# Weight loads moved into the stage in front, last quad's shift on ScalarE with the routing sums, and the expert choice handed over inside its own stage

## What is computed

```python
h = _layernorm(x, axis=-1) * (1 + ca) + sa
x = x + ga * attn(h, ...)
h = _layernorm(x, axis=-1) * (1 + cb) + sb
x = x + gb * ffn(h, ...)
```

```python
main = jax.nn.gelu(x @ W1m + b1m) @ W2m + b2m
logits = jnp.mean(x, axis=1) @ w_gate + b_gate
probs = jax.nn.softmax(logits, axis=-1)
top_vals, top_idx = lax.top_k(probs, K)
gate_w = top_vals / jnp.sum(top_vals, axis=-1, keepdims=True)
...
a = jnp.clip(alpha, 0.1, 1.0)
return a * main + (1.0 - a) * expert_out
```

## Time and profile before

| | us |
|---|---|
| median of 3 runs | 6144.11 |
| lowest and highest of the runs | 6137.29, 6147.71 |
| the profiled execution's own time | 6168.16 |
| its span | 6166.0 |
| mean granted PE clock in it | 0.899 of full |

### The profile page before, as it was taken

The page is one execution under the profiler, slowest core; times in us unless marked ns, Lnnn a source line. Parts: engine busy times, 40 slices in busy tenths (PEclk is TensorE's granted clock), DMA queues, the critical chain, the costliest instruction groups (busy, mean ns, idle before and its releaser), DMA issues. The chain is left out here.

```text
span 6166.0 us, 105844 instructions
## 1 busy us (share of the span) xinstructions
PE 5082.9 (82%) x38207; PEld 2620.5 (42%) x38217; DVE 3501.2 (57%) x5633; ACT 3147.4 (51%) x7104; POOL 2512.3 (41%) x2126
## 2 busy tenths in 40 slices
PE   6999779888876999988999998874237999874995
PEld 2444334344433666643566663342112222241784
DVE  5777422487744666643666654565338999730233
ACT  2666633366663666642566663342014888831542
POOL 3333100222206888841788871116562232116025
PEclk7999989899997999998999999986557999976997
DMA  3343111133310000011000000011112333211123
GB/s 99 108 120 110 40 45 48 57 111 103 108 44 20 6 7 8 5 56 45 6 8 6 6 3 4 2 28 41 36 32 65 95 89 96 59 46 49 52 76 90
DMA packets 329515, 312.95 MB, mean 51 GB/s; under 512 B 78758, under 2 KB 279106, under 8 KB 327106
## 3 DMA queue, kind: packets, MB, share of 16 engines
q1 hardware_dynamic: 312642, 285.77, 16.2%
q0 software_dynamic: 16384, 20.69, 1.2%
HBM read 172.15 MB, written 136.32 MB: 50 GB/s over the span
## 5 line engine op out<-in xcount | busy, mean ns | idle before, releaser
L784 ACT ACTIVATE a_prob<-a_PB 128x512 f32<-128x512 f32 x2304 | 1253.4, 598 | 456.9 <-PE a_PB L626 342.7
L674 PE MATMUL a_PO<-a_prob,a_V 128*32 128x256 f32 (+3 forms) x8192 | 715.0, 422 | 22.6 <-ACT a_cn L757 22.3
L938 DVE TENSOR_REDUCE a_blocks<-a_PA 128x8 f32<-128x1024 f32 x512 | 602.0, 1214 | 37.4 <-PE a_PA L626 35.0
L941 DVE TENSOR_REDUCE a_neg<-a_PA 128x2 f32<-128x1024 f32 x512 | 590.8, 1212 | 34.8 <-PE a_PA L639 34.7
L639 PE MATMUL a_PA<-a_KS,a_QS 48*128 48x512 bf16 (+3 forms) x3072 | 469.0, 344 | 112.9 <-DVE a_blocks L938 71.0
L2538 DVE TENSOR_REDUCE f1a_neg<-f1a_PA 128x2 f32<-128x384 f32 (+1 forms) x512 | 266.7, 521 | 488.4 <-PE f1a_PA L2340 487.9
L2468 POOL TENSOR_TENSOR f1a_prob<-f1a_prob,f1a_inv 128x384 f32<-128x384 f32 (+1 forms) x512 | 394.2, 773 | 283.3 <-DVE f1a_inv L2542 283.3
L656 PE MATMUL a_PB<-a_QS,a_KS 51*128 51x512 bf16 (+3 forms) x3072 | 448.3, 329 | 56.6 <-ACT a_prob L784 54.9
L2432 ACT ACTIVATE f1a_pt<-f1a_PT 128x512 f32<-128x512 f32 (+1 forms) x512 | 278.7, 544 | 348.5 <-PE f1a_PT L2349 344.7
L2425 ACT ACTIVATE f1a_prob<-f1a_PA,f1a_neg 128x192 f32<-128x192 f32 (+1 forms) x1024 | 405.3, 404 | 67.9 <-DVE f1a_neg L2538 67.8
L639 PEld LDWEIGHTS a_PA<-a_KS,a_QS 48*128 48x128 bf16 x3072 | 123.5, 94 | 635.5 <-DVE a_blocks L938 199.6
(11 more groups left out here) (416 smaller groups left out, 10391.4 us busy)
## 6 DMA issues: line engine op xcount, KB each, us to landing
a_spill<-a_qkp SPq DMA_DIRECT2D x96, 384.0 KB
a_QS<-a_spill SPq DMA_DIRECT2D x384, 96.0 KB, 2.5
a_KS<-a_spill SPq DMA_DIRECT2D x384, 96.0 KB, 2.5
a_spill<-a_qkp SPq DMA_DIRECT2D x96, 256.0 KB
a_raw<-a_cn SPq DMA_DIRECT2D x192, 72.0 KB
a_spill<-a_qkp SPq DMA_DIRECT2D x96, 128.0 KB
f_rows<-tokens_in SPq DMA_DIRECT2D x78, 128.0 KB
tokens_out<-f_rows SPq DMA_DIRECT2D x78, 128.0 KB
```

The costliest lines, as they stand in the source:

```text
L674: mm = nc.tensor.matmul(PO[32 * j:32 * j + 32, first:last], V[:, par, t, 8 * e + pr], prob[:, k % st.ring, e, c + first - q0:c + last - q0 ...
L784: nc.scalar.activation(prob[:, k % st.ring, e], PB[:, ring_b.slot(0, ("b", s, e))], ACT.Exp, scale=scale).then_inc(pb_used, 1)
L938: nc.vector.tensor_reduce(to, of, AX, ALU.max).then_inc(pa_used, 1)
L941: nc.vector.tensor_reduce(neg[:, t, pr], PA[:, bank:bank + 2], AX, ALU.max, negate=True).then_inc(pa_used, 1)
```

## The change

Four things, in the seven norm stages, the routing and four weight-loading stages:

1. `norm_phase` gets a program for SP, which runs an optional `fetch` and waits for it at the stage's end. With it `n0b` loads the main expert and the three routing tiles, `f1n0` and `f1n1` load the GLU weights, and `n2a` loads the wide head's. The tiles are allocated around both stages, and the stages behind lose their loads and the waits on `loaded`.
2. In the six norms without `sums`, POOL adds the shift for batches 0 to 11 and ACT for the last quad.
3. In `n0b` (with `sums`) ACT adds all the shifts: quad 0 behind the copy of batch 11, quads 1 to 3 behind the last root. Each of them also writes the sum over the tokens (`accum_out`) to `route_sums`, and L1071 is gone.
4. The write to DRAM and the read back of the expert choice move from the end of the routing stage to the start of `f0`. SP reads the indices first and then the weights, and waits for both before it loads an expert; DVE waits for both before its first work in `f0`; PE and ACT wait for neither.

```diff
-def norm_phase(net, name, layer, part, small=None):
+def norm_phase(net, name, layer, part, small=None, fetch=None, sums=None):
...
+        fetched = nc.alloc_semaphore(name + "fetched")
...
+        def shift_of(b):
+            return shift[:, b:b + 1] if small is None else net.ln[:, 1, small:small + 1]
+
+        @block.sync
+        def _(sp):
+            if fetch is not None:
+                loads = fetch(sp, fetched)
+                sp.wait_ge(fetched, 16 * loads)
...
+            def add_shift(q):
+                for b in range(4 * q, 4 * q + 4):
+                    act.wait_ge(scaled, b + 1)
+                    if sums is None:
+                        nc.scalar.activation(H[:, b], h0[:, b % 4], ACT.Identity, bias=shift_of(b))
+                    else:
+                        nc.scalar.activation(H[:, b], h0[:, b % 4], ACT.Identity, bias=shift_of(b),
+                                             accum_out=sums[:, b:b + 1]).then_inc(shifted, 1)
+
             for b in range(B):
                 act.wait_ge(centered, b + 1)
                 at_least(act, variance, 4 * (b // 4 - 1))
@@ -259,7 +278,11 @@
                 nc.scalar.activation(xs[:, b], xc[:, b % 3], ACT.Copy).then_inc(taken, 1)
                 if b % 4 == 0 and b:
                     root(b // 4 - 1)
+                if b == 11 and sums is not None:
+                    add_shift(0)
             root(GROUPS - 1)
+            for q in (1, 2, 3) if sums is not None else (3,):
+                add_shift(q)
...
-            for b in range(B):
+            for b in range(B - 4 if sums is None else 0):
                 pool.wait_ge(scaled, b + 1)
-                s = shift[:, b:b + 1] if small is None else net.ln[:, 1, small:small + 1]
-                nc.gpsimd.tensor_tensor(H[:, b], h0[:, b % 4], s.broadcast_to([P, S]), ALU.add).then_inc(shifted, 1)
+                nc.gpsimd.tensor_tensor(H[:, b], h0[:, b % 4], shift_of(b).broadcast_to([P, S]), ALU.add).then_inc(shifted, 1)
...
-        @block.sync
-        def _(sp):
-            sp.dma_start(wg[:], d["f0_wg"]).then_inc(loaded, 16)
-            sp.dma_start(bg[:, 0], d["f0_bg"].partition_broadcast(B)).then_inc(loaded, 16)
-            sp.dma_start(alpha[:], d["f0_alpha"].partition_broadcast(B)).then_inc(loaded, 16)
-            sp.wait_ge(routed, 1)
-            sp.dma_start(w_dram, w[:]).then_inc(out1, 16)
-            sp.dma_start(i_dram, index[:, 0, 0:2]).then_inc(out1, 16)
-            sp.wait_ge(out1, 32)
-            sp.dma_start(net.w3[:], w_dram.rearrange("b k -> (b k)").partition_broadcast(P)).then_inc(out2, 16)
-            sp.dma_start(net.chosen[:], i_dram.rearrange("b (k o) -> o (b k)", o=1)).then_inc(out2, 16)
-            sp.wait_ge(out2, 32)
-
         @block.tensor
         def _(pe):
-            pe.wait_ge(loaded, 48)
-            pe.wait_ge(means, 2)
+            pe.wait_ge(means, 1)
             nc.tensor.matmul(ps[0:B, 0:E8], hm[:], wg[:], start=True, stop=True).then_inc(logit, 1)
...
-            nc.vector.tensor_reduce(hm[:], net.H[:], AX, ALU.add).then_inc(means, 1)
-            dve.wait_ge(means, 1)
-            nc.vector.tensor_scalar(hm[:], hm[:], 1.0 / S, None, ALU.mult).then_inc(means, 1)
+            nc.vector.tensor_scalar(hm[:], net.route_sums[:], 1.0 / S, None, ALU.mult).then_inc(means, 1)
...
-        w1 = sb("w1", [P, NU, F4 * P])
-        w2 = sb("w2", [P, NU, F4, P])
-        bias = sb("bias", [P, NU, F4 + 1])
+        w1, w2, bias = net.f0_w1, net.f0_w2, net.f0_bias
+        w_dram = nc.dram_tensor("r0_w_dram", [B, 3], F32, kind="Internal").ap()
+        i_dram = nc.dram_tensor("r0_i_dram", [B, 2], U32, kind="Internal").ap()
...
         @block.sync
         def _(sp):
-            sp.dma_start(w1[:, 0], d[name + "w1m"]).then_inc(loaded, 16)
-            sp.dma_start(w2[:, 0], d[name + "w2m"].rearrange("(t p) n -> p t n", p=P)).then_inc(loaded, 16)
-            sp.dma_start(bias[:, 0], d[name + "bm"]).then_inc(loaded, 16)
+            sp.dma_start(w_dram, net.route_w[:]).then_inc(choice_out, 16)
+            sp.dma_start(i_dram, net.route_index[:, 0, 0:2]).then_inc(choice_out, 16)
+            sp.wait_ge(choice_out, 32)
+            sp.dma_start(net.chosen[:], i_dram.rearrange("b (k o) -> o (b k)", o=1)).then_inc(choice_in, 16)
+            sp.dma_start(net.w3[:], w_dram.rearrange("b k -> (b k)").partition_broadcast(P)).then_inc(choice_in, 16)
+            sp.wait_ge(choice_in, 32)
 
             def batch(b, par):
...
         @block.tensor
         def _(pe):
-            pe.wait_ge(loaded, 48)
 
...
         @block.scalar
         def _(act):
-            act.wait_ge(loaded, 48)
...
         def _(dve):
-            dve.wait_ge(loaded, 48)
+            dve.wait_ge(choice_in, 32)
...
-        @block.sync
-        def _(sp):
-            sp.dma_start(w[:], d[name + "w"].rearrange("j p n -> p j n")).then_inc(loaded, 16)
-
         @block.tensor
         def _(pe):
-            pe.wait_ge(loaded, 16)
...
         @block.sync
         def _(sp):
-            sp.dma_start(w1[:], d["f1_w1"][l].rearrange("p (j n) -> p j n", n=P)).then_inc(loaded, 16)
-            sp.dma_start(w2[:], d["f1_w2"][l].rearrange("(j p) n -> p j n", p=P)).then_inc(loaded, 16)
-            sp.dma_start(b1[:], d["f1_b1"][l]).then_inc(loaded, 16)
-            sp.dma_start(b2[:], d["f1_b2"][l]).then_inc(loaded, 16)
             if not last:
                 sp.wait_ge(zeroed, 1)
...
         @block.tensor
         def _(pe):
-            pe.wait_ge(loaded, 64)
...
@@ -2720,9 +2705,22 @@
         for l in range(2):
             with nc.cleanup_on_exit():
                 local_attention_phase(net, f"f1a{l}_", l)
-            with nc.sbuf_tensor(f"N{l}", [P, B, S], F32) as net.N:
+            with ExitStack() as own:
+                net.N = own.enter_context(nc.sbuf_tensor(f"N{l}", [P, B, S], F32))
+                net.glu_w1 = own.enter_context(nc.sbuf_tensor(f"glu{l}_w1", [P, 2 * GLU, P], F32))
+                net.glu_w2 = own.enter_context(nc.sbuf_tensor(f"glu{l}_w2", [P, GLU, P], F32))
+                net.glu_b1 = own.enter_context(nc.sbuf_tensor(f"glu{l}_b1", [P, 2 * GLU], F32))
+                net.glu_b2 = own.enter_context(nc.sbuf_tensor(f"glu{l}_b2", [P, 1], F32))
+
+                def fetch(sp, fetched):
+                    sp.dma_start(net.glu_w1[:], net.d["f1_w1"][l].rearrange("p (j n) -> p j n", n=P)).then_inc(fetched, 16)
+                    sp.dma_start(net.glu_w2[:], net.d["f1_w2"][l].rearrange("(j p) n -> p j n", p=P)).then_inc(fetched, 16)
+                    sp.dma_start(net.glu_b1[:], net.d["f1_b1"][l]).then_inc(fetched, 16)
+                    sp.dma_start(net.glu_b2[:], net.d["f1_b2"][l]).then_inc(fetched, 16)
+                    return 4
+
                 with nc.cleanup_on_exit():
-                    norm_phase(net, f"f1n{l}_", 1, 1, small=l)
+                    norm_phase(net, f"f1n{l}_", 1, 1, small=l, fetch=fetch)
                 with nc.cleanup_on_exit():
                     glu_phase(net, f"f1g{l}_", l, last=(l == 1))
 
@@ -2771,21 +2769,43 @@
             modulation_phase(net)
         with nc.cleanup_on_exit():
             heads16_phase(net, "a0_", 0, causal=True, rope=True, w_sum=False)
-        with nc.cleanup_on_exit():
-            norm_phase(net, "n0b_", 0, 1)
-        with nc.cleanup_on_exit():
-            route_batches_phase(net)
-        with nc.cleanup_on_exit():
-            mlp_phase(net, "f0_", 0, 3)
+        with ExitStack() as own:
+            def sb(n, shape, dt=F32):
+                return own.enter_context(nc.sbuf_tensor(n, shape, dt))
+
+            net.route_wg, net.route_bg, net.route_alpha = sb("route_wg", [P, E8]), sb("route_bg", [B, 1, E8]), sb("route_alpha", [B, 1])
+            net.route_index, net.route_w, net.route_sums = sb("route_index", [B, 1, E8], U32), sb("route_w", [B, 3]), sb("route_sums", [P, B])
+            net.f0_w1, net.f0_w2, net.f0_bias = sb("f0_w1", [P, 3, F4 * P]), sb("f0_w2", [P, 3, F4, P]), sb("f0_bias", [P, 3, F4 + 1])
+
+            def fetch_main(sp, fetched):
+                sp.dma_start(net.route_wg[:], d["f0_wg"]).then_inc(fetched, 16)
+                sp.dma_start(net.route_bg[:, 0], d["f0_bg"].partition_broadcast(B)).then_inc(fetched, 16)
+                sp.dma_start(net.route_alpha[:], d["f0_alpha"].partition_broadcast(B)).then_inc(fetched, 16)
+                sp.dma_start(net.f0_w1[:, 0], d["f0_w1m"]).then_inc(fetched, 16)
+                sp.dma_start(net.f0_w2[:, 0], d["f0_w2m"].rearrange("(t p) n -> p t n", p=P)).then_inc(fetched, 16)
+                sp.dma_start(net.f0_bias[:, 0], d["f0_bm"]).then_inc(fetched, 16)
+                return 6
+
+            with nc.cleanup_on_exit():
+                norm_phase(net, "n0b_", 0, 1, fetch=fetch_main, sums=net.route_sums)
+            with nc.cleanup_on_exit():
+                route_batches_phase(net)
+            with nc.cleanup_on_exit():
+                mlp_phase(net, "f0_", 0, 3)
         with nc.cleanup_on_exit():
```

(13 more changed lines are left out.)

28 lines of the change are left out of this document (8 added, 20 removed).

## The result

The changed kernel takes **6120.7 us** (median of seven runs, 6113.4 to 6131.5) against 6144.1 before (6137.3 to 6155.0): a ratio of 0.9959, with an interval from 0.9947 to 0.9970, so 25 us less (18 to 33). Two repeats of the same comparison gave 0.9948 (0.9935 to 0.9962) and 0.9948 (0.9930 to 0.9966), each on another chip. The forecast was 6111.0, a ratio of 0.9946, in a range of 6101 to 6122. Sign and range held; the first comparison is 10 us short of the forecast, the two repeats are not.

The account below looks back on a forecast made before the run. No engine bounds the whole kernel; stages differ, with dead time at norm ends, weight-load starts and routing. Terms 8.3 + 0.8 + 8.65 + 2.9 + 12.5 = 33.1 us, off 6144.1, gave 6111.0, range 6101 to 6122.

Parts of the forecast that it names:

- Tails of six norms: Ends of six norms: ACT takes POOL's last quad and ends 0.75 us behind DVE, 1.38 us each, 8.3 us together.
- Tail of `n0b`: End of `n0b`: ACT adds with accumulator reads and ends earlier, 0.8 us won, between 0.4 and 1.2.
- The price of nothing: Middle of `n0b`: quad 0's additions on ACT cost nothing, covered by DVE's 1.91 us idle; otherwise up to 3.6 us.
- Routing: Routing stage: removing the sum at L1071 takes 8.69 us off the only path; counted as 8.65 us.
- Start of `f0`: First expert's product in `f0` comes 5.1 us earlier, less 2.2 for a second cold start: 2.9 us, ends 2.7 and 5.1.
- Start of three more stages: GLU 0, GLU 1 and wide head: PE no longer waits for loads, 4.47, 5.29 and 2.70 us, together 12.5.
- nothing is added: Starts of both GLU stages and wide head: PE cold before and cold again, so no extra cost, 0 us.
- (a): Stage starts: another wait of PE replaces the load wait, 6117 us, or 6123.5 if all 12.5 stayed; chance 9%.
- (b): `f0`: the clock stays up over the idle time, gain 5.1 instead of 2.9 us, total 6108.8; chance 8%.
- (c): Norm tails: ACT reloads its table for the new additions, 1.28 us in each of seven, total 6120; chance 2%.
- (d): `f0`: PE stays at the lower clock after its second start, total 6156 us or more; chance 2%.
- (e): Untouched stages run otherwise against the clock's changes; a loss of 21 us or more hides the gain, about 6135; chance 4%.

Follow-up runs that it names:

- The part alone: Only the last quad's shift moved from POOL to ACT in all seven norms, against the kernel before: 5964.7 us, ratio 0.9983.
- the trace where the yardstick was 18.32: Whole change, third time, against the kernel before: 6124.8 us, ratio 0.9948; yardstick: routing's last result to first product of L1155 (L1157 after the change).
- the fillers in the hole: Twenty useless products on PE in f0's idle stretch, added to the changed kernel and nothing else: 5948.4 us in one run (before on that chip: 5973.8).
- the three traces of the table: Stage-by-stage traces of the whole change, unaltered, against two of the kernel before; measured 6120.7, 5944.2 and 6124.8 us, ratios 0.9959, 0.9948 and 0.9948.
- The products in the norm: Useless bf16 products on PE in the last third of every norm, added to the changed kernel: 6118.3 us, ratio to before 0.9935.

## Why the prediction came out as it did

**Tails of six norms: right.** Forecast 1.38 each, from ACT 0.75 us behind DVE. It is 0.75 to 0.76 us in the six norms of the changed kernel. The part alone gave 10 us in total against 9.7 expected with `n0b`'s part.

**Tail of `n0b`: right within its bounds, at the upper one.** The read of the accumulator overlaps but for the last, so the tail shrank by 2.13 - 0.98 = 1.15 us; I had taken 0.8 between 0.4 and 1.2. One sign that I had named failed: DVE's idle time of 1.91 us before the reciprocal of quad 3 did not shrink, it vanished (762.20 has no bracket). The working had a slip there: 3.6 us behind 761.96 is 765.6, not 765, so the reciprocal of quad 2 could have come 2.3 us late, more than the cover of 1.91. The price of nothing held only because ACT's additions were cheaper than the 0.91 us taken: in the middle of the norm the four with their reads hold ACT up for 2.8 us (751.89 to 754.71), 0.7 each. They did push DVE, by the new wait of 0.56 us at 756.38. Before quad 3 the cover was then used up but not exceeded: ACT's root ends at 761.41 + 0.69 = 762.10 in the changed kernel, and DVE goes from its product to the reciprocal at 762.20 without a pause.

**Routing: right.** Forecast 8.65. From DVE's first instruction to the last result it was 797.10 - 784.84 = 12.26 us and is 778.41 - 774.78 = 3.63: 8.63 less.

**Start of `f0`: the mechanism was right, two sizes were off.** Forecast 2.9, measured 19.0 - 17.0 = 2.0 to 2.1 us. The step "the expert's last tile is issued at 805.09", 7.99 us behind the last result, came true to 0.03 us (786.37 - 778.41 = 7.96; 8.1 and 8.5 in the other two traces of it). The step "lands 2.6 us later" failed: PE started 3.48 us behind that issue (786.37 to 789.85), and 2.6 and 3.4 us behind it in the other two traces. I had taken the median over all 32 loads of the stage for the first one. So the hole was 5.0 us long, not 3.7, and by the prediction's own sign ("wrong if that hole is longer" than 3 to 4 us) this step failed. The second cold start came, and cost 5.40 - 3.70 = 1.7 us here, where the lower level lasted 3.4 us, and 6.57 - 3.70 = 2.9 in the trace where the yardstick was 18.32 and it lasted 6.8; I had taken 2.2. The Trainium skill ("TensorE: Matmul & The Clock Gate", section "HAM oscillation — how this bites in real kernels") was right against this edit, and the fillers in the hole show the size of it. What I had not weighed is that leaving the hand-over outside would have brought as much: the edit won 6 us in PE's start and paid them back in the hole and in the second cold start.

**Start of three more stages: the waits were right, "nothing is added" failed.** The time from DVE's end to PE's start shrank by 16.6 us over the three (16.9 in the first pair of traces) against 12.5 + 3 x 1.38 = 16.6 forecast. But the stages themselves grew by 2.5, of which 2.3 in the two GLU stages. "PE was cold at these starts and will be cold again, so nothing is added" took both cold starts for equally long. With the old starts the GLU stages ran at the lower level for 3.5 to 5.1 us (eight starts in four traces, mean 4.0). With the new ones it was 3.0 to 6.2 us (fourteen starts in seven traces, mean 5.0), 5.9 in the mean of the three traces of the table. Each us more at the lower level costs half a us. So the three traces of the table lie above the rest: over all seven with the new starts the two GLU stages take 256.6 us in the mean, over the four with the old ones 255.5, which makes the term 1.1 us and not 2.3.

The granted clock shows where the level comes from. It does not fall at the GLU stage's first product; it has fallen in the norm, 15.4 to 17.0 us before that product with the old starts and 9.5 to 12.4 us before it with the new ones. The whole stretch at the lower level lasted 20.5 us at each of the eight old starts, 17.1 at eleven of the new ones and 13.7 at three. PE's start comes some 6 us earlier and the stretch ends 3.4 us earlier at eleven starts and 6.8 at three, so mostly more of it lies behind the start. The products in the norm remove it: at five of the six GLU starts behind them the clock is full well before the first product, at the sixth from 1.3 us before it. What decides between 13.7 and 17.1 us was not tried.

**The sum.** 33.1 forecast, 31.9 by the stages, 31 and 33 us by the two later comparisons, 25 by the first. Added up from what the steps measured it is less: six tails 8.2, `n0b` 1.15, routing 8.6, `f0` 2.1, the waits 12.5, less 2.3 in the GLU stages, together 30.3. The other 1.6 of the 31.9 no step explains; they are within what traces scatter (`n0b` alone took 44.0 us in one trace of before and 41.0 in the other), so that the stages came so near the forecast is in part luck. The first comparison's interval ends at 33. The profiled pair of the first comparison can't decide it: its spans differ by 47.5 us, of which only 34.0 lie in the touched stages. The 10 us between forecast and first result stay open, as scatter that I can't assign. (The low end of the sum, 31.2, does not follow from the bounds given for its terms; they give 31.85.)

**The rivals.** (a) fell: PE starts 0.76 us behind ACT. (b) fell: the clock is at 0.56 in the first 2 us behind the hole, and the eight products there take 5.40 us. (c) fell: ACT's table is loaded at 774.74 and 779.11, at the stages' starts, and nowhere in a norm's tail; the kernel has 24 table loads before and after. (d) fell: the product behind them, L1157, takes its 3.60 us, the time at full clock, and `f0` as a whole has a clock of 0.99 as before:

```profile
779.20:1128.00 348.80, 338.17 (x768) 145.05 (x768) 74.89 (x96) 133.19 (x193) 0.00 (x0) 0.99 0.17 49
```

(e) fell as a large effect: the untouched attention stages differ by -0.6 us in the means. But one of them, behind an unchanged border, is longer, which the prediction had named as a sign against it. The second local-attention stage takes either 832.4 to 833.1 us or 835.2 to 836.1. It was the short time in both traces of the kernel before, and the long one in all three of the changed kernel, 3.4 us more; the kernels with a part of the change, or with something added to it, show both. Whether the change makes the long one likelier can't be said from these; if it does, it costs up to 3.4 us. The difference lies in one stretch, from 60 to 120 us behind its start. First the changed kernel, 836.1 us, then the one with the hand-over undone, 832.6 us (windows, columns as above):

```profile
2911.10:2971.10 60.00, 56.44 (x364) 34.61 (x363) 35.21 (x71) 35.89 (x108) 45.83 (x33) 0.90 0.04 9
```

```profile
2910.00:2970.00 60.00, 56.44 (x397) 35.40 (x395) 38.55 (x77) 37.66 (x114) 48.43 (x34) 0.97 0.04 10
```

PE is busy for the same time and has 33 more products in it, at a clock of 0.97 instead of 0.90.

## What to carry to other kernels

Between two stages, look at what the last engine to end does there and give its tail to an engine that follows closer; load the next stage's weights one stage early. The waits that go can be read off the timeline to some tenths of a us; what the clock then does at the earlier start can't, and took 1 to 2 us back here. A wait that is only moved behind PE's first work turns into a hole, and PE started cold behind it: before handing something over "inside", sum the hole and the second cold start against running through later. Where PE has little to do ahead of a stage that it bounds, products of no use kept the clock up (3 us for each GLU stage). But they must end before the other engines do, and behind another idle stretch they made the next start slower. Split waits keep a small read off the path of what needs another one.
